# Two of seven group masks made by ScalarE instead of VectorE

## The reference

```
gi = sum(|x|[..., None] <= thresholds, axis=-1)      # 8 thresholds
idx = min(gi, 7); d = deltas[idx]; zp = zero_points[idx]
xq = clip(round(x / d) + zp, 0, 63); cond = where(gi == 8, 0, (xq - zp) * d)
# first block: router logits of cond pick the top 2 of 4 rank-16 adapters
logits = cond @ router_w.T;  gates = softmax(top2(logits))
x = x + sum_e gates[e] * (cond @ A[e].T) @ B[e].T * 4
# second block: two dense products, each with low-rank terms
y = x @ W.T + (x @ lora_A[label]) @ lora_B.T * 0.5
x = x + y @ kernel + bias + (adapters picked by gate, and shared ones) of y
```

## Time and profile before

| | |
|---|---|
| median of 3 runs | 488.16 us (486.01 to 490.64) |
| the profiled execution: time, span | 489.24 us, 487.5 us |
| TensorE busy | 471.8 us (97%) |
| VectorE busy | 391.4 us (80%) |
| ScalarE busy | 356.6 us (73%) |
| mean granted clock of TensorE | 0.979 |

### The profile page before, as it was taken

The page is one execution under the profiler, slowest core; times in us unless marked ns, Lnnn a source line. Parts: engine busy times, 40 slices in busy tenths (PEclk is TensorE's granted clock), DMA queues, the critical chain, the costliest instruction groups (busy, mean ns, idle before and its releaser), DMA issues.

```text
span 487.5 us, 5645 instructions
## 1 busy us (share of the span) xinstructions
PE 471.8 (97%) x2200; PEld 365.7 (75%) x2200; DVE 391.4 (80%) x381; ACT 356.6 (73%) x297; POOL 6.8 (1%) x12
## 2 busy tenths in 40 slices
PE   6989999999889999999999999999999999999896
PEld 5963788887648888787777777787787768767774
DVE  3289978789979989939879989798799994999400
ACT  3779987864978398676699599776899697776001
POOL 0000000001000001000000000000000000000000
PEclk9599999999999999999999999999999999999799
DMA  8975542313301527030441316014214013102002
GB/s 281 422 267 178 171 142 73 90 43 98 107 0 37 181 86 204 13 108 1 151 141 44 108 54 200 38 55 130 108 54 152 0 55 129 56 0 86 1 0 87
DMA packets 35500, 50.61 MB, mean 104 GB/s; under 512 B 26610, under 2 KB 26866, under 8 KB 33074
## 3 DMA queue, kind: packets, MB, share of 16 engines
q1 hardware_dynamic: 34322, 41.87, 26.7%
q0 software_dynamic: 1152, 8.39, 4.8%
HBM read 39.51 MB, written 10.49 MB: 103 GB/s over the span
## 4 chain that ended last, share of the span: by engine, by line
PE 76%; DVE 16%; issue 4%; DMA 2%; ACT 1%; SPq 0%; DVEq 0%; ACTq 0%
PE bank L965 10%; PE bank L966 10%; PE bank L967 10%; DVE val L615 7%; PE bank L848 6%; PE bank L942 5%; PE bank L874 5%; PE bank L917 5%; PE bank L913 5%; PE bank L914 4%; PE bank L896 3%; DVE inside L608 3%; PE bank L814 3%; DVE val L598 2%; DMA la<-la_in 2%
## 5 line engine op out<-in xcount | busy, mean ns | idle before, releaser
L406 ACT ACTIVATE val<-level,shift,small 128x2048 f32<-128x2048 int16 x64 | 133.8, 2091 | 16.3 <-DVE val L615 16.2
L615 DVE COPY_PREDICATED val<-inside,val 128x2048 f32<-128x2048 uint8 x56 | 141.3, 2523 | 0.3
L395 ACT ACTIVATE level<-xq,inv 128x2048 int16<-128x2048 f32 x64 | 127.9, 1998 | 2.0 <-DMA xq<-xt_in 1.4
L598 DVE TENSOR_SCALAR val<-val,width,unshift 128x2048 f32<-128x2048 f32 x64 | 86.0, 1347 | 22.7 <-ACT val L406 22.4
L965 PE MATMUL bank<-p_hi,x_hi 128*128 128x512 f32 x256 | 102.5, 401 | 0.0
L966 PE MATMUL bank<-p_lo,x_hi 128*128 128x512 f32 x256 | 100.4, 392 | 0.0
L967 PE MATMUL bank<-p_hi,x_lo 128*128 128x512 f32 x256 | 100.4, 392 | 0.0
L608 DVE TENSOR_SCALAR inside<-absx,thr 128x2048 uint8<-128x2048 f32 x56 | 71.4, 1285 | 7.1 <-ACT absx L387 7.1
L965 PEld LDWEIGHTS bank<-p_hi,x_hi 128*128 128x128 f32 x256 | 48.5, 189 | 17.6 <-issue 8.8
L966 PEld LDWEIGHTS bank<-p_lo,x_hi 128*128 128x128 f32 x256 | 48.4, 189 | 10.5 <-issue 0.5
L967 PEld LDWEIGHTS bank<-p_hi,x_lo 128*128 128x128 f32 x256 | 48.3, 189 | 10.5
(11 more groups left out here) (91 smaller groups left out, 477.4 us busy)
## 6 DMA issues: line engine op xcount, KB each, us to landing
xq<-xt_in POOLq DMA_DIRECT2D x8, 1024.0 KB, 5.8
xs<-xt_in SPq DMA_DIRECT2D x8, 1024.0 KB, 4.9
out_t<-ost SPq DMA_DIRECT2D x16, 512.0 KB, 3.0
wst<-w_in SPq DMA_DIRECT2D x14, 512.0 KB, 3.6
la<-la_in SPq DMA_DIRECT2D x4, 512.0 KB, 10.4
kst<-k_in SPq DMA_DIRECT2D x4, 512.0 KB, 13.9
lb<-lb_in SPq DMA_DIRECT2D x1, 2048.0 KB, 18.7
kst<-k_in SPq DMA_DIRECT2D x1, 2048.0 KB, 7.9
```

What stands on the lines that cost most here:

```text
L395: nc.scalar.activation(level[:, g % 2], xq[:, c % 2], ACT.Copy, scale=inv[:, g:g + 1]).then_inc(levels_made, 1)
L406: nc.scalar.activation(val[:, turn(c, g)], level[:, g % 2], ACT.Relu, bias=shift[:, g:g + 1], scale=par[:, 1, g:g + 1]).then_inc(raised, 1)
L598: nc.vector.tensor_scalar(v, v, width[:, g:g + 1], unshift[:, g:g + 1], ALU.min, ALU.add).then_inc(valued, 1)
L615: nc.vector.copy_predicated(val[:, acc(c)], inside[:, g % 2], val[:, turn(c, g)]).then_inc(merged, 1)
```

## The change

Masks 3 and 6 of each batch leave VectorE. ScalarE makes them: Sign(edge - |x|), where edge is the threshold times 1 + 1.5 * 2^-24, so that the result is 1 where |x| <= threshold and -1 above, which the uint8 tile holds as 0. The instruction stands in ScalarE's `quant(c, g)` ahead of levels(c, g+1), and waits for |x|, for edge and for merge(c, g-2). VectorE's counter of masks is renumbered for the five that it keeps, and merge waits for the right one of the two counters. VectorE makes `edge` once at the start. The two other groups of waits, values and merges stay as they were.

```diff
--- before.py
+++ after.py
@@ -105,6 +105,7 @@
     par = small[:, 0:3 * G].rearrange("p (a g) -> p a g", a=3)
     gate_rep, gsel = small[:, 3 * G:3 * G + BATCH], small[:, 3 * G + BATCH:]
     thr, _ = place("thr", [P, G], F32)
+    edge, _ = place("edge", [P, G], F32)
     inv, _ = place("inv", [P, G], F32)
     shift, _ = place("shift", [P, G], F32)
     unshift, _ = place("unshift", [P, G], F32)
@@ -186,6 +187,7 @@
     ofull, p_hi_made, ofree = sem("ofull"), sem("p_hi_made"), sem("ofree")
     abs_made, levels_made, raised = sem("abs_made"), sem("levels_made"), sem("raised")
     valued, masked, merged, q_made = sem("valued"), sem("masked"), sem("merged"), sem("q_made")
+    act_masked, thr_made, edge_made = sem("act_masked"), sem("thr_made"), sem("edge_made")
     mid_made, gate_step, gap_made, exp_made = sem("mid_made"), sem("gate_step"), sem("gap_made"), sem("exp_made")
     gates_made = sem("gates_made")
     mg_made, mgt_full, mgt_made = sem("mg_made"), sem("mgt_full"), sem("mgt_made")
@@ -227,6 +229,11 @@
     OUT = {c: at for at, c in OUT.items()}
     OUT_AT = OUT
     OUT = {at: c for c, at in OUT_AT.items()}
+
+    ACT_MASKS = (3, 6)
+
+    def dve_masks(c, g):
+        return c * (G - 1 - len(ACT_MASKS)) + g - sum(m <= g for m in ACT_MASKS)
 
     XAT, ZAT = (1, 3), 4
 
@@ -406,8 +413,17 @@
                 nc.scalar.activation(val[:, turn(c, g)], level[:, g % 2], ACT.Relu, bias=shift[:, g:g + 1],
                                      scale=par[:, 1, g:g + 1]).then_inc(raised, 1)
 
+            def mask(c, g):
+
+                act.wait_ge(edge_made, 1)
+                act.wait_ge(abs_made, c + 1)
+                act.wait_ge(merged, c * (G - 1) + g - 2)
+                nc.scalar.activation(inside[:, g % 2], absx, ACT.Sign, bias=edge[:, g - 1:g], scale=-1.0).then_inc(act_masked, 1)
+
             def quant(c, g):
 
+                if g in ACT_MASKS:
+                    mask(c, g)
                 if g + 1 < G:
                     levels(c, g + 1)
                 elif c + 1 < BATCH:
@@ -609,7 +625,10 @@
 
             def merge(c, g):
                 dve.wait_ge(valued, c * G + g + 1)
-                dve.wait_ge(masked, c * (G - 1) + g)
+                if g in ACT_MASKS:
+                    dve.wait_ge(act_masked, c * len(ACT_MASKS) + ACT_MASKS.index(g) + 1)
+                else:
+                    dve.wait_ge(masked, dve_masks(c, g))
                 if g >= 2:
                     dve.wait_ge(merged, c * (G - 1) + g - 1)
                 nc.vector.copy_predicated(val[:, acc(c)], inside[:, g % 2], val[:, turn(c, g)]).then_inc(merged, 1)
@@ -624,7 +643,7 @@
                 value(c, g)
                 if g == 1:
                     mask(c, 1)
-                if g and g + 1 < G:
+                if g and g + 1 < G and g + 1 not in ACT_MASKS:
                     mask(c, g + 1)
                 if g:
                     merge(c, g)
@@ -655,8 +674,10 @@
             nc.vector.memset(warm, 1.0).then_inc(warm_made, 1)
             nc.vector.memset(ones.bitcast(F32), 1.0).then_inc(ones_made, 1)
             dve.wait_ge(small_in, 16)
-            nc.vector.max(thr, par[:, 0])
+            nc.vector.max(thr, par[:, 0]).then_inc(thr_made, 1)
             nc.vector.reciprocal(inv, par[:, 1])
+            dve.wait_ge(thr_made, 1)
+            nc.vector.scalar_tensor_tensor(edge, thr, 1.5 * 2.0 ** -24, thr, ALU.mult, ALU.add).then_inc(edge_made, 1)
             nc.vector.tensor_scalar(width, par[:, 1], LEVELS, None, ALU.mult)
             nc.vector.tensor_tensor(shift, par[:, 1], par[:, 2], ALU.mult).then_inc(table_step, 1)
             dve.wait_ge(table_step, 1)
```

## The result

| | before | after |
|---|---|---|
| median, 4 runs each | 488.44 us | 499.62 us |
| range | 486.01 to 490.64 | 499.23 to 502.74 |
| profiled execution: time, span | 489.24, 487.5 us | 499.45, 497.7 us |

The ratio after to before is 1.0237 (95% interval 1.0191 to 1.0282): slower, by 11.2 us in the medians and 10.2 us between the two profiled executions. That is clear of the noise; whether it is more than 2% the interval leaves open. The forecast was 495.5 us, in a range from 489.5 to 501.0.

A forecast was written before the change was run, and what follows sets the result against it. TensorE, busy 97% of the span, was taken to bound the kernel, with stretches where VectorE, ScalarE behind it, decides. Terms 4.8 + 0.8 + 1.6 = 7.2 us on the median of 488.16 gave 495.5 us, range 489.5 to 501.

The forecast's parts named there:

- What it swaps: Sixteen masks, whole run: each costs ScalarE 1.9 us and frees 1.2 us of VectorE, plus 30 and minus 19 us.
- The wait that comes with it: ScalarE's queue: mask, levels and raise all follow merge(c, g-2), 5.8 us where it was 2.0, 3.8 more.
- A to C: Groups (0,3), (0,6), (1,3), (1,6): 2.4 + 2.4 + 0.1, less a rounding, 4.8 us later at the second half of K'.
- Part B: Group (1,3): w_hi comes 3.8 us later, VectorE saves 1.2, leaving 2.6 us, or 2.4 with the queue's rounding.
- D: Batches 2 to 6: TensorE waits 0.8 us for batch 5's values, bounds 0 and 1.5; other batches end ahead of TensorE.
- E: Last batch: value(7,6) starts late behind mask, levels and raise, so the batch ends 1.6 us later, bounds 1.0 and 2.2.
- Sum: Whole kernel: 4.8 + 0.8 + 1.6 = 7.2 us, giving 495.5 us; bounds 4.4 to 9.3 us, so 492.6 to 497.5.
- The clock rival: Longer TensorE wait near 124 us lowers the granted clock, costing up to 4.5 us, 2 to 3 unspared: 498.5; chance 0.14.
- a wait near 147 us: Sign in the profile after: TensorE's wait there has grown, its second half of P starting near 147.6 us.
- Table loads: ScalarE: Sign needs another table set than Exp, up to 16 loads, four on the path, 5.1 us: 500.5; chance 0.10.
- VectorE's pace: VectorE decides at 89 to 142 and 413 to 454 us, so freeing it wins: 480 us; chance 0.08.
- Hidden slack: Unseen slack halves the early loss and batches 2 to 6 cost nothing: 2.4 + 0 + 1.6, 492 us; chance 0.18.

The follow-up runs named there:

- Experiment 4: Changed kernel with all sixteen ScalarE masks, each moved behind levels and raise_levels of its group: 490.60 us, ratio 1.0057 to the kernel before.
- experiment 1: Kernel before with only masks 3 and 6 of batches 0 and 1 moved to ScalarE, placed as in the change: 493.03 us, ratio 1.0104.
- experiment 6: Kernel before with one mask, (1,3), moved to ScalarE ahead of levels(1,4): 490.48 us, ratio 1.0063.
- Experiment 9: Kernel before with only masks 3 and 6 of batches 2 to 6 moved to ScalarE, placed as in the change: 489.03 us, ratio 1.002.
- experiment 7: Changed kernel with 13 unused matmuls in TensorE's wait for the last batch's values, and the `mgt_made` wait put ahead of them: 495.04 us, ratio 1.0168 to before.
- experiment 8: Kernel before with 5 unused matmuls in TensorE's wait for the last batch's values, and the `mgt_made` wait put ahead of them: 486.03 us, ratio 0.9954.
- experiment 2: Kernel before with only masks 3 and 6 of batch 7 moved to ScalarE, placed as in the change: 493.22 us, ratio 1.0093.
- experiment 5: Changed kernel with all sixteen ScalarE masks, each between levels and raise_levels of its group: 496.88 us, ratio 1.0195 to the kernel before.
- experiment 3: Changed kernel with the sixteen masks made by no engine, merges using the flags standing in the buffer: 484.79 us, ratio 0.9952 to the kernel before.
- experiment 10: Kernel before with one mask, (7,7), moved to ScalarE behind its raise: 486.41 us, ratio 0.9957.
- experiment 11: Kernel before with three masks, (1,6), (1,7) and (7,7), moved to ScalarE behind their raises: 483.43 us, ratio 0.9906.

## Why the prediction was right, and where its size was off

The direction, the mechanism and the places were right. The size, 7.3 us against the old median, was short of 11.2. My bounds for the three parts, 492.6 to 497.5 us, did not hold the measured 499.62; the range did, because its upper end had been set at 501 for the rivals of clock and tables. That it held is therefore in part luck: the forecast had no term for what was missing.

**What it swaps.** Right for ScalarE: 1997 ns against the assumed 1998, plus 29.6 us. VectorE's 375.7 us missed both figures of the prediction, minus 19 us in the text and 371 among the signs (which takes off sixteen whole records of 1285 ns); the time doesn't hang on it.

**The wait that comes with it.** Right: 5.8 us from the end of merge(1,1) to w_hi where it was 2.0. Experiment 4 shows that the place is the cause: the same load behind the raise costs a quarter by the ratios and a third by the marks.

**A to C, 4.8 us.** Measured 5.2 in the change and 5.3 in experiment 1. Part B alone is 2.7 (experiment 6) against my 2.4 or 2.6. What I called rounding in the queue walk was the error; the distances by hand, 2.6 + 2.6 + 0.1, were right.

**D, 0.8 us.** This term was too small: 1.9, above its upper bound of 1.5. The wait at batch 5's products is 0.9, as forecast (369.30 is 7.56 later, the products of batch 4 6.68 later). But 0.3 goes to products that run longer behind a wait, and 0.7 came in between the products of batches 1 and 2. Of that, 0.4 is TensorE's wait for bet_lo. The high part of bet stands in ScalarE's queue behind the mask (2,6); I had looked for loss at the products alone. The other 0.3 I can't place. Experiment 9 shows 1.8 as well, without the masks of batches 0, 1 and 7.

**E, 1.6 us.** Measured 2.3, above its upper bound of 2.2. The 1.6 at value(7,6) are there as 1.7: value(7,6) starts 5.9 us after the start of ScalarE's pass at 447.87, where it was 4.2 after the one at 439.46. What I left out is upstream: mask (7,3) delays zt, for which TensorE now waits 0.3 us, and bu starts 26.23 us after batch 6's products where it had 25.66, 0.6 more. I had said that the wait for bu absorbs that mask; it absorbs all but what the mask does to TensorE first.

**Sum.** 5.2 + 1.9 + 2.3 = 9.4 against 7.2, and 0.7 of the profiled executions' difference lies ahead of levels(0,3). That start lies between 34.98 and 37.44 us over the thirteen traces, with no order by kernel, so it isn't the change's.

**The medians.** 9.4 isn't 11.2. My sum was built on one execution of before, in which the clock had fallen at the end. Experiments 7 and 8 show that this is 3.3 us, that the kernel before pays it only in part of its executions, and that it is gone in both traces with a filled wait. All three traces with a last wait of 3 us and nothing in it (the change, experiments 2 and 5) show it. If the kernel before pays in half to two thirds of its executions, an estimate from experiment 8 and its times (and a loose one, see there), the difference comes to 9.4 + 3.3 x (1/3 to 1/2) = 10.5 to 11.1.

**The rivals.** The clock rival was right about the place and wrong about the price. The wait near 124 us grew to 4.0, and the clock did fall behind it: sixteen products took 5.38 us in place of 3.69. But that is 1.7 us, where rival 1 had reckoned with up to 4.5, and the 1.8 us to spare covered it: from kp_hi to the products of batch 1 it takes 12.96 us where it took 12.88. So one of my signs, a wait near 147 us that has grown, failed too: that wait is gone. What the clock did cost came behind the last wait, where I had no term for it. Table loads: none beyond the one. VectorE's pace: refuted by experiments 2 and 3. Hidden slack: no part was smaller than forecast.

## What to carry to other kernels

When work moves to a less busy engine, look at what stands behind it in that engine's queue and at what the moved step waits for: here a pass of 1.9 us cost 3.8, because it pulled a pass that had run inside a wait to the far side of that wait. Put the moved step behind the one that others wait for, and move it only where the engine would wait next; three masks placed so won 4.6 us, sixteen that all went ahead of levels lost 11. Before moving, leave the step out once to see what its removal wins with the rest of the schedule as it is (2.3 us here). And follow every step that stands behind it in the queue, not only the one you have in mind: bet and zt brought 0.4 and 0.6 us that I had not looked for.

## What the hardware showed that I had not expected

**A clock that falls behind a wait in some executions.** Behind the last wait of 3.1 us, the granted clock of the kernel after by stretch:

```profile
458.00:464.00 6.00, 3.96 (x18) 2.95 (x16) 5.93 (x4) 0.00 (x0) 0.00 (x0) 1.00 0.17 69
464.00:470.00 6.00, 4.98 (x28) 4.98 (x28) 0.97 (x1) 0.00 (x0) 0.00 (x0) 0.67 0.01 3
```

It was 1.00 through the wait and 0.67 in the stretch behind it. So TensorE went from 2.4 to 1.2 GHz behind it. Six traces have a last wait of 1.1 to 1.3 us: in the kernel before the products behind it took 5.71 us, in experiments 1, 3, 4, 6 and 9 3.79. Three traces have a wait of 3.0 to 3.1, all with products of 6 us or more. Three have at most 0.4 (experiments 8, 10, 11), all with 3.79. The Trainium skill, page "TensorE: Matmul & The Clock Gate", section "Part 1: The HAM clock gate", says that an array that was idle gets half the rate, and that the same kernel shows cold stretches of different length from run to run. The products at 1.6 to 2 times their length, and one trace in six with the fall, agree.

**The same at the first waits, where it is mostly free.** Behind the wait for u near 124 us the sixteen products took 5.1 to 5.4 us in place of 3.69 in nine of the thirteen traces: in all four with a wait of 3.3 to 4.0 us (the change, experiments 1, 6 and 7) and in five of seven with 2.2 to 2.3 us (experiments 2, 4, 5, 8 and 9, but not the kernel before and experiment 10). Experiments 3 and 11, with at most 1.3 us of waiting, have 3.69. In each of the nine, TensorE's wait for kp_lo near 142 us is 0.3 us or none, where it was 1.8, and from kp_hi to the products of batch 1 it takes 12.86 to 12.96 us, with 12.88 before. So the lower clock took little more than the next wait would have taken.

It can also fall at the wait near 142 us. In experiment 10 the stretch behind it, 1.8 us of waiting before it, shows 0.60, and the stretch behind the last wait 1.00; in the other twelve traces there is no fall between 142 and 150 us:

```profile
144.00:148.00 4.00, 3.94 (x11) 3.16 (x12) 4.00 (x7) 3.95 (x9) 0.00 (x0) 0.60 0.01 4
...
458.00:464.00 6.00, 6.00 (x39) 5.35 (x39) 2.32 (x13) 0.21 (x1) 0.00 (x0) 1.00 0.00 0
```

That cost about 1.6 us in that one execution (14.49 us from kp_hi to the products of batch 1, against 12.88 before) and may be part of that kernel's spread.

**Products behind a wait** of 0.3 to 1.3 us take 3.79 us at the full clock (experiments 1, 3, 4, 6 and 8 to 11) where 32 products in a dense stream take 3.52.
